# Stages of four chunks each, and a last stage whose last ten steps in t are loaded by pairs of chunks

## The reference, cut to what matters

```python
# x: (1024, 24, 1024) = (B, T, S) f32, W1: (S, T), W2: (S, S)
h = jax.nn.sigmoid(jnp.einsum('bts,st->bs', x, W1) + b1)
return h @ W2.T + b2
```

## Time and profile before

| | us |
|---|---|
| median of 3 runs | 315.55 (315.52 to 315.67) |
| the profiled execution's own time | 316.05 |
| its span, first to last instruction | 314.3 |
| PE busy | 262.0 (83%) |
| DVE busy | 247.3 (79%) |
| POOL busy | 214.9 (68%) |
| ACT busy | 50.9 (16%) |
| x and W read | 104.97 MB, 347 GB/s over the span |

### The profile page before, as it was taken

The page is one execution under the profiler, slowest core; times in us unless marked ns, Lnnn a source line. Parts: engine busy times, 40 slices in busy tenths (PEclk is TensorE's granted clock), DMA queues, the critical chain, the costliest instruction groups (busy, mean ns, idle before and its releaser), DMA issues.

```text
span 314.3 us, 4779 instructions
## 1 busy us (share of the span) xinstructions
PE 262.0 (83%) x1761; PEld 223.9 (71%) x1761; DVE 247.3 (79%) x368; ACT 50.9 (16%) x85; POOL 214.9 (68%) x125
## 2 busy tenths in 40 slices
PE   0957768658889999999799999858999977989994
PEld 0946758558767888888678888746888876667773
DVE  0639998729998988889977888868887897788665
ACT  4111213202262100100600000040111113000020
POOL 3128766635469999994999977479988749994000
PEclk9989999969999999999799999979999999999999
DMA  7999999999999999999999999999999999996007
GB/s 214 392 389 387 386 387 387 401 388 386 387 387 385 386 387 387 387 385 381 373 373 373 385 384 382 376 384 373 374 373 374 368 351 339 344 348 202 2 0 268
DMA packets 67675, 109.48 MB, mean 348 GB/s; under 512 B 3642, under 2 KB 40514, under 8 KB 67652
## 3 DMA queue, kind: packets, MB, share of 16 engines
q1 hardware_dynamic: 67056, 107.06, 95.7%
q10 hardware_dynamic: 596, 2.11, 1.7%
HBM read 104.97 MB, written 4.19 MB: 347 GB/s over the span
## 4 chain that ended last, share of the span: by engine, by line
PE 50%; DMA 32%; DVE 5%; issue 5%; SPq 4%; ACT 2%; DVEq 0%; ACTq 0%
DMA ring<-in_r_x 32%; PE xbank L232 25%; PE pbank L301 20%; DVE acc L354 3%; PE xbank L332 3%; SPq L195 3%; SPq L201 2%; PE pbank L291 1%; ACT h L431 1%; DVE w_lo L361 1%; PE pbank L332 1%; ACT h_hi L456 1%; PE pbank L261 0%; ACT L431 0%; DVE acc L352 0%
## 5 line engine op out<-in xcount | busy, mean ns | idle before, releaser
L354 DVE SCALAR_TENSOR_TENSOR acc<-xbank,w,acc 128x512 f32<-128x512 f32 x280 | 200.4, 746 | 40.6 <-PE xbank L232 35.1
L232 PE MATMUL xbank<-ident,ring 128*128 128x128 f32 x1184 | 176.1, 284 | 44.3 <-DMA ring<-in_r_x 34.7
L232 PEld LDWEIGHTS xbank<-ident,ring 128*128 128x128 f32 x1184 | 146.5, 147 | 76.7 <-issue 30.7
L485 POOL TENSOR_TENSOR nat<-nat,w1all 128x768 f32<-128x768 f32 (+2 forms) x56 | 106.9, 1910 | 60.6 <-DMA nat<-in_r_x 47.8
L495 POOL TENSOR_TENSOR nat<-nat 128x768 f32<-128x768 f32 (+2 forms) x46 | 87.6, 1905 | 3.6
L301 PE MATMUL pbank<-w_lo,h_hi 128*128 128x512 f32 x112 | 48.8, 435 | 0.0
L301 PE MATMUL pbank<-w_hi,h_hi 128*128 128x512 f32 x112 | 48.5, 433 | 0.0
L301 PE MATMUL pbank<-w_hi,h_lo 128*128 128x512 f32 x112 | 41.0, 431 | 0.0
L431 ACT ACTIVATE h<-acc,b1col 128x512 f32<-128x512 f32 (+1 forms) x22 | 12.5, 600 | 99.7 <-DVE acc L354 64.0
L348 DVE TENSOR_SCALAR acc<-xbank,w 128x512 f32<-128x512 f32 x16 | 11.9, 748 | 13.8 <-PE xbank L232 11.6
L443 ACT COPY y<-pbank 128x512 f32<-128x512 f32 x16 | 9.4, 587 | 79.3 <-PE pbank L301 79.3
(11 more groups left out here) (37 smaller groups left out, 93.2 us busy)
## 6 DMA issues: line engine op xcount, KB each, us to landing
ring<-in_r_x SPq DMA_DIRECT2D x38, 1024.0 KB, 13.3
ring<-in_r_x SPq DMA_DIRECT2D x36, 768.0 KB, 11.1
nat<-in_r_x SPq DMA_DIRECT2D x20, 512.0 KB, 13.2
nat<-in_r_x SPq DMA_DIRECT2D x24, 384.0 KB, 11.5
ring<-in_r_x SPq DMA_DIRECT2D x18, 512.0 KB, 8.1
y<-in_L_rec_W SPq DMA_DIRECT2D x2, 2048.0 KB, 15.1
nat<-in_r_x SPq DMA_DIRECT2D x12, 256.0 KB, 8.7
out_y<-y ACTq DMA_DIRECT2D x4, 512.0 KB, 7.1
```

The costliest lines, as they stand in the source:

```text
L232: mm = pe.transpose(xbank[u % XBANKS][:, j * P:(j + 1) * P], tile, ident[:, :])
L354: nc.vector.scalar_tensor_tensor(out=total, in0=bank, scalar=weight, in1=total, op0=ALU.mult, op1=ALU.add).then_inc(unit_added, 1)
L485: nc.gpsimd.tensor_tensor(slot, slot, row, ALU.mult).then_inc(nat_weighed, 1)
```

## The change

There are four stages of 4 chunks. Block 1 has 4 and 4 chunks instead of 3, 3 and 2, so all natural loads are 512 KB and the whole-stage items 1024 KB. Pool takes 5 t in the last stage (4, 6, 6 before it). In the last stage the items t = 5 to 13 have all 4 chunks; the last ten t are loaded twice by pairs: (t, chunks 0 and 1) for t = 14 to 23, then (t, chunks 2 and 3) for t = 14 to 23, 512 KB each. The last stage's natural sum is turned in the first of these passes, before t = 21.

The products now go by groups: one for each of the first three stages, and two of a pair of chunks each in the last stage. In the last stage the steps of stage 2 are spread over the units 8 to 59, where the first pair ends; the first pair's 48 steps, less REST, over the units 64 to 79; REST is 14 and follows the last unit. The second pair's products are the tail. The first pair's sigmoids and splits are made by ACT and Pool in full width, as in the other stages; the quarters are left to the second pair. ACT now waits for the products of stage 2 before all sigmoids of the last stage.

```diff
 STAGES = (
-    (0, 0, 4, 4, (2, 3, 5, 7, 9, 11, 13, 15, 17, 18), "keep"),
-    (0, 4, 4, 6, (0, 2, 3, 5, 6, 8, 9, 11, 12, 14, 15, 17), "last"),
-    (4, 0, 3, 6, (0, 2, 3, 5, 6, 8, 9, 11, 12, 14, 15, 17), "keep"),
-    (4, 3, 3, 6, (0, 2, 3, 5, 6, 8, 9, 11, 12, 14, 15, 17), "add"),
-    (4, 6, 2, 6, (0, 2, 3, 5, 6, 8, 9, 11, 12, 13), "last"),
+    (0, 0, 4, (2, 3, 5, 7, 9, 11, 13, 15, 17, 18), "keep"),
+    (0, 4, 6, (0, 2, 3, 5, 6, 8, 9, 11, 12, 14, 15, 17), "last"),
+    (4, 0, 6, (0, 2, 3, 5, 6, 8, 9, 11, 12, 14, 15, 17), "keep"),
+    (4, 4, 5, (0, 1, 3, 4, 6, 7, 9, 11), "last"),
 )
+NC = 4
+SPLIT = 10
...
-    REST = 12
+    REST = 14
+    PAIR = NC // 2
+    loads = [[(t, 0, NC) for t in range(pools[i], T)] for i in range(NS)]
+    loads[LAST] = [(t, 0, NC) for t in range(pools[LAST], T - SPLIT)]
+    loads[LAST] += [(t, c, PAIR) for c in (0, PAIR) for t in range(T - SPLIT, T)]
...
+        order = [("x", t, c0 + c) for t, c0, n in loads[i] for c in range(n)]
+        at = order.index(("x", T - 2, 0)) if i < LAST else order.index(("x", T - 3, 0))
+        units.append(order[:at] + [("n", 0, c) for c in range(NC)] + order[at:])
...
+    PAIR_END = units[LAST].index(("x", T - 1, PAIR - 1)) + 1
+    groups = [(i, 0, NC) for i in range(LAST)] + [(LAST, 0, PAIR), (LAST, PAIR, PAIR)]
+    gfate = fate[:LAST] + ["add", "last"]
...
+        def steps_due(g, i, v):
+            steps = OUTS * steps_of(g)
+            if g == i - 1:
+                lead = 2 * NC
+                span = (len(units[i]) * 4 // 5 if i < LAST else PAIR_END) - lead
+            elif i == LAST and g == LAST:
+                lead = PAIR_END + 2 * PAIR
+                span = len(units[i]) - lead
+                steps -= REST
+            else:
+                return 0
             return max(0, min(steps, -(-(v - lead + 1) * steps // span)))
...
         @block.tensor
...
-                    if i > 0:
-                        for k in range(steps_due(i, v - 1) if v else 0, steps_due(i, v)):
-                            product_step(i - 1, k)
-            last_steps = OUTS * steps_of(LAST - 1)
+                    for g in range(max(i - 1, 0), i + 1):
+                        for k in range(steps_due(g, i, v - 1) if v else 0, steps_due(g, i, v)):
+                            product_step(g, k)
+            last_steps = OUTS * steps_of(LAST)
             for k in range(last_steps - REST, last_steps):
-                product_step(LAST - 1, k)
-            for c in range(chunks[LAST]):
+                product_step(LAST, k)
+            for c in range(PAIR, NC):
...
         @block.vector
...
+                    for g in range(max(i - 1, 0), i + 1):
+                        if gfate[g] != "keep" and v >= 2:
+                            for n in range(outs_due(g, i, v - 2), outs_due(g, i, v - 1)):
+                                add_out(g, n, pbank[n % 2])
-            for c in range(chunks[LAST]):
+            for c in range(PAIR, NC):
                 for j in range(JT):
...
                     nc.vector.tensor_copy(h_hi[:, c, rows], h[:, c, rows]).then_inc(tail_hi, 1)
...
                     nc.vector.tensor_tensor(h_lo[:, c, rows], h[:, c, rows], h_hi[:, c, rows].bitcast(F32),
                                             ALU.subtract).then_inc(tail_lo, 1)
-            for n in range(outs_due(LAST, len(units[LAST]) - 2), OUTS):
-                add_out(LAST - 1, n, pbank[n % 2])
+            for n in range(outs_due(LAST, LAST, len(units[LAST]) - 2), OUTS):
+                add_out(LAST, n, pbank[n % 2])
             for n in range(OUTS):
-                add_out(LAST, n, xbank[(UNITS + n) % XBANKS] if n < XBANKS else pbank[n - XBANKS])
+                add_out(NS, n, xbank[(UNITS + n) % XBANKS] if n < XBANKS else pbank[n - XBANKS])
...
         @block.scalar
...
                 if i > 0:
-                    act.wait_ge(h_lo_ready, first_h[i])
+                    act.wait_ge(h_lo_ready, NC * i)
                     act.wait_ge(out_summed, OUTS * i)
...
-                    if i < LAST:
+                    if i < LAST or c < PAIR:
...
         @block.gpsimd
...
+            low_parts(LAST)
```

More of the change, by code:

```diff
@@ L65, in rec_kernel, with item_at @@
+    added_at = [OUTS * sum(f != "keep" for f in gfate[:g]) for g in range(NS + 1)]
     item_of, item_end = {}, []
     for i in range(NS):
-        for t in range(pools[i], T):
-            item_of[i, t] = len(item_end)
-            item_end.append(first_unit[i] + units[i].index(("x", t, chunks[i] - 1)))
+        for t, c0, n in loads[i]:
+            item_of[i, t, c0] = len(item_end)
+            item_end.append(first_unit[i] + units[i].index(("x", t, c0 + n - 1)))
+    def item_at(i, t, c):
+        return (item_of[i, t, c], 0) if (i, t, c) in item_of else (item_at(i, t, c - 1)[0], item_at(i, t, c - 1)[1] + 1)
@@ L71, in rec_kernel, with unit_before @@
+    def unit_before(i, v):
+        same = [w for w in range(v) if units[i][w][2] == units[i][v][2]]
+        return same[-1] if same else None
     parts = [(i, k, f) for i in range(NS) for k in range(pools[i]) for f in range(2)]
@@ L74, in sum_turned @@
     def sum_turned(i):
-        return first_unit[i] + units[i].index(("n", 0, chunks[i] - 1)) + 1
+        return first_unit[i] + units[i].index(("n", 0, NC - 1)) + 1
     def sums_made(m):
@@ L101, in rec_kernel @@
         y = sb("y", [P, JT, O])
[L102 to L105, removed]
+        acc = sb("acc", [P, NC, BANK])
+        h = sb("h", [P, NC, BANK])
+        h_hi = sb("h_hi", [P, NC, BANK], F32R)
+        h_lo = sb("h_lo", [P, NC, BANK], F32R)
         w1all = sb("w1all", [P, NK, S])
@@ L153, in out_half, with steps_of, outs_due @@
             return j, slice(oh * BANK, (oh + 1) * BANK)
[L155 to L167, removed]
+        def steps_of(g):
+            return 3 * groups[g][2] + (gfate[g] == "keep")
+        def steps_due(g, i, v):
[9 more added lines that the diff above has]
+                return 0
             return max(0, min(steps, -(-(v - lead + 1) * steps // span)))
-        def outs_due(i, v):
-            return steps_due(i, v) // steps_of(i - 1)
+        def outs_due(g, i, v):
+            return steps_due(g, i, v) // steps_of(g)
         EARLY, SETN = 1 + NK0, 1 + 2 * NK
@@ L185, in _ @@
             m = 0
-            for i, (j0, c0, n, _, places, _) in enumerate(STAGES):
-                for at in range(T - pools[i]):
+            for i, (j0, s0, _, places, _) in enumerate(STAGES):
+                for at, (t, c0, n) in enumerate(loads[i]):
                     if at in places:
@@ L275, in product_step @@
                 if r == 0:
[L276 removed]
+                    if g == 0 and n == 0:
                         pe.wait_ge(w_lo_ready, OH * SC)
@@ L332, in _ @@
                         mm = pe.matmul(bank[:, :], a[:, c, j * P:(j + 1) * P], w[:, STAGES[LAST][1] + c, cols],
-                                       start=c == 0 and k == 0, stop=c == chunks[LAST] - 1 and k == 2)
-                    if c == chunks[LAST] - 1:
+                                       start=c == PAIR and k == 0, stop=c == NC - 1 and k == 2)
+                    if c == NC - 1:
                         mm.then_inc(out_summed, 1)
@@ L494, in add_sum, with low_parts @@
                     pool.wait_ge(nat_added, sums_made(m - 2))
[L495 to L499 removed]
+                nc.gpsimd.tensor_tensor(slot, slot, nat[:, (m - 2) % NATS, :, :], ALU.add).then_inc(nat_added, 1)
+            def low_parts(g):
+                i, c0, n = groups[g]
+                for c in range(c0, c0 + n):
+                    pool.wait_ge(h_hi_ready, NC * i + c + 1)
                     nc.gpsimd.tensor_tensor(h_lo[:, c, :], h[:, c, :], h_hi[:, c, :].bitcast(F32),
```

117 lines of the change are left out of this document (52 added, 65 removed).

## The result

| | before | changed |
|---|---|---|
| median, us | 315.53 (315.38 to 315.67, 4 runs) | 322.26 (320.54 to 323.40, 4 runs) |
| the profiled execution's own time | 316.05 | 323.40 |
| its span | 314.3 | 321.6 |
| PE busy | 262.0 | 265.8 |
| DVE busy | 247.3 | 250.1 |

The ratio is 1.021, with a 95% interval of 1.019 to 1.023. Measured once more later, the same kernel came out at 321.60 (320.55 to 322.58), 1.0187 (1.0169 to 1.0205). It is slower, and the prediction of 320.4 (316.8 to 322.9) holds the time. The profiled execution is the slowest of the first four; its own time is the one to hold against its span.

What follows compares the result with a forecast made beforehand. Loads set the pace, with TensorE close behind. R 296.1, steps and drain 14.35, stall 3.4, clock 1.2 and the end 4.1 give span 319.2; plus 1.75, less 0.5: 320.4 us (316.8 to 322.9).

Steps and rivals of the forecast that it cites:

- R: Moment when the last stage's units are all turned and only REST steps and tail are left; forecast 296.1, before 295.08.
- the fourth rival: Last stage's start: TensorE still at half clock when products start, or natural sum late; up to 1.5 us, 322 to 323.5; 12%.
- Part 1: Block 1's loads: wider rows move at 387 GB/s instead of 373 and 374, so loads could end 4.3 us earlier.
- Part 2: Start of the last stage: the x load of unit 8, the first unit with products, lands at 231.5.
- Part 3: TensorE in the last stage: 47.3 + 1.75 + 0.6 + 14.9 = 64.6 us from unit 8, beside loads that then stop binding.
- Part 4: Tail: output 5's add stands behind DVE's eight cast-and-subtract pairs until R + 5.3, stalling TensorE 3.4 us; a 1.2 us gap goes.
- The sign given for the tail: End of the kernel: 17 to 18.5 us from R to the last product.
- Part 5: TensorE's clock after the tail's stall: idling brings it down, price 1.2 us, own range 0 to 1.6.
- What follows the last product: End of the kernel, from the last product to the end of the span: 4.1 us.
- The first rival: Last stage: loads set the end after all, R 290.8, time 313.9, faster; 5%.
- the second: Tail: no stall, if output 5 were added before the pairs; stall and clock go, 315.8; 4%.
- the third: Block 1's loads: row size makes no difference, they stay at 374, last stage starts 2.7 us later, 323.1; 3%.

Runs made afterwards that it cites:

- experiment 1: Changed kernel, but DVE adds output 5 of pair 1 before its eight cast-and-subtract pairs, not behind them: 316.74 us, ratio 1.0039 to before.
- experiment 9: The changed kernel measured once more, unchanged: 321.60 us (320.55 to 322.58).
- experiment 4: Changed kernel without the 32 product steps h_lo x w_hi of stage 2's group, loads and units unchanged: 319.04 us, ratio 1.0106.
- experiment 5: As experiment 1, with 18 of stage 2's 104 product steps done behind unit 3 of the last stage: 314.87 us, ratio 0.9978 to before.
- experiment 3: Changed kernel with REST = 6 instead of 14: 317.92 us, ratio 1.0076.
- experiment 2: Changed kernel with the add of output 5 between DVE's fourth and fifth cast-and-subtract pair: 318.75 us, ratio 1.0098.
- experiment 7: As experiment 1, with only the last six t loaded by pairs (12 loads of 512 KB instead of 20): 321.59 us, ratio 1.0191.

## Why the prediction was right

The order of events that it gave for the tail, and that TensorE and not the loads would set R, were right, and its miss of 1.9 us is in two sizes. That 322.3 still lies in the range is in part luck: the loss by the clock, 2.7, lies outside the 0 to 1.6 that its own range allowed, and R, 297.44, at the edge of the 295 to 297.5. The range reached 322.9 because of the fourth rival, which had little part in it.

- *Part 1, the rows' length.* The rates came as forecast: 386 to 396 GB/s in the stages that had 373. The rule that the Trainium skill states (page "DMA: Bandwidth & Descriptors", Specifications: line rate from 512 B on) is not what is seen: with 2 KB rows in the same stages the rate went up by 3.5%. The DMA share was full at every level (in the kernel before 1.05 at 388 GB/s over 60 to 90, 1.06 at 372 over 230 to 250, 1.07 at 344 over 257 to 285), so the DMA engines moved less in the same busy time. The size of a load changed together with its rows (768 KB to 1 MB), and no run parts the two. The gain did not arrive at the end, as forecast.
- *Part 2, the start of the last stage.* Unit 8 was to come at 231.5; its turn came at about 231.7, and in experiment 1 at 231.47. The clock was low just then (0.68 over 230 to 235), and still was when the products started. This is the fourth rival's event, against which the prediction held that both dips before had ended in time; it came in four of the seven profiles named in experiment 1, and its price was not up to 1.5 us but 0.3, for with the full clock TensorE waits for loads instead. In experiment 9, with the same dip, all of the stage's start is 0.95 earlier, so this much the start varies.
- *Part 3, TensorE in the last stage.* 64.6 us from unit 8 to R were forecast, 65.7 measured. R came at 297.44 instead of 296.1: 0.2 from the start, 0.8 from units 8 to 59 (unit 60 begins at 279.79, 48.1 us behind unit 8 instead of 47.3), 0.4 from the rest (17.65 instead of 17.25; the wait for h_hi was to be 0.6 and is 0.48). The 47.3 was a misreading: the stretch in the earlier trace rows is 47.6 long, and the 0.62 of idling stands before it, so nothing was to come off. Beyond that, "so they go together" put TensorE's waits for loads at nothing; in experiment 1, where the clock held, they are 0.26 at 235.54 and again at 239.60, and R is 297.09. Experiments 4 and 5 show that it is TensorE's work that counts here: taking work away or moving it forward brings R earlier, with the loads unchanged.
- *Part 4, the tail.* Right. The stall was to be 3.4 us and is 3.20, the release R + 5.3 and is R + 5.2; the last unit was added and the pairs began at R + 0.75, both as forecast. ACT's quarters were done at 299.59, R + 2.15. Experiment 1 shows the cause by taking it away, experiment 3 by another way. The sign given for the tail, 17 to 18.5 us from R to the last product, failed: it was 20.4. It did not fit the prediction's own sum either, whose terms make 19.0 (14.35 + 3.4 + 1.2).
- *Part 5, the clock.* Right that it would fall, mis-sized: 1.2 was taken from 24 transposes at a stage's start, and it is 2.7. The term went wrong because a price was carried over from another place. There too TensorE was at work all the time at the low clock, but the low stretch was shorter: from about 153.8 to 157.2, and from the resuming at 209.11 to about 211.8, against 5.7 us of work here (302.63 to 308.34). In it 13 distances between products took 5.7 us instead of 3.0. Why the low stretch is longer here, no run shows.
- *What follows the last product* was 3.8 instead of 4.1.

Together: + 1.3 (R), - 0.2 (stall), + 1.5 (clock), - 0.3 (end) is 2.3 of the 2.4 us between the forecast span of 319.2 and 321.6. The first rival (the loads set the end after all) is ruled out by slices 32 to 34 and experiment 4; the second (no stall) by the trace; the third (the loads of block 1 stay at 374) by the slices. Both sizes were off to the same side, which is why the time came out in the upper part of the range.

What the change would have been worth without its stall is experiment 1: 316.7, still 1.1 above the kernel before measured beside it. The wider loads were 3.5 us ahead at 249.2, but 138 steps and 80 units stood in the last stage, and TensorE, not the loads, carried them. Only with the 18 early steps does the split pay, by 0.2%.

## What to carry to other kernels

When work is split so that one half's results are used while the other half runs, read each engine's program as a queue and look for the release of a shared buffer that now stands behind the other half's work: one add of 0.7 us, put behind 3.7 us of casts, cost 3.2 us and 2.7 more for the clock. Here TensorE was nearly as busy as the loads, and faster loads gave nothing until its work was moved into the holes in which it still waited for them. And steps spread over fewer units need their adds as close behind: an even plan became slow once each output took 1.4 units. When one stretch of such a plan is made longer, look at both sides: the stretch that got thinner now waits for loads, the one that got denser for adds.

## What the runs showed of the hardware

An idle time of 3.2 us of TensorE in the middle of dense products came with a fall of its granted clock to 0.50 in all three profiles that have it (the changed kernel twice, and experiment 4). In the profile of the changed kernel the clock fell some 2 us after the last product had ended, and came back in the window from 308, 5.7 us after the products had resumed at 302.63. With 1.35 us of idling in the same place it stayed at 1.00. At the lower level a product of 128 x 128 by 128 x 512 began 0.43 us behind the one before, against 0.23 at the higher. At the stage starts of the kernel before, the low stretches had lasted some 3 us.

Between these two lengths the idle time alone does not say what the clock does. Where the last stage starts, TensorE idled 2.6 to 2.7 us, turned four units and idled once more, 2.13 us where the clock was still up. By then or just behind, the clock had fallen in five profiles (the changed kernel twice, experiments 2, 4 and 7) and stayed at 1.00 in two (experiments 1 and 3).
